# Two layer norms whose mean is taken off by matmuls with a centering matrix, in a four-block image kernel on one core

## Chip, cores and metric

The program runs on one core of one Trainium2 chip. It is one launch, and the metric is the device time in microseconds (us) of one execution. Engines: PE (TensorE, matmuls), DVE (VectorE), ACT (ScalarE), POOL (GpSimd), and SP, which here only issues DMAs. Each engine runs its own instructions in order and waits at semaphores for the others.

## What is computed

The input x has 8 images of 32 x 32 pixels and 64 channels (C). Four blocks follow, each added to x or taken from it after a group norm `_gn`. The third one matters here:

```python
def layer_norm(x, g, b, eps=1e-05):
    mu = jnp.mean(x, axis=-1, keepdims=True)
    var = jnp.var(x, axis=-1, keepdims=True)
    return (x - mu) / jnp.sqrt(var + eps) * g + b
...
x_norm = layer_norm(x_flat, ln_g, ln_b)          # over the 64 channels of a pixel
y = mamba_block(x_norm, in_proj_w, ..., out_proj_w)   # projections, selective scan, y @ out_proj_w.T
y = y + skip_scale * x_norm
y = layer_norm(y, ln_g, ln_b)
y = y @ proj_w.T + proj_b
...
x = x + _L0_conv_ref(_gn(x), ...)    # 5 steps of a diffusion with depthwise convolutions
x = x + _L1_conv_ref(_gn(x), ...)    # 3 x 3 convolution
x = x + _L2_conv_ref(_gn(x), ...)    # the block above
x = x + _L3_conv_ref(_gn(x))         # 2D DCT
```

So there are two layer norms over the channels: g = 0 ahead of the projections, and g = 1 behind the scan.

## The kernel before

Two images fill the 128 partitions (2 x 64 channels), a pair of images is a tile of 128 x 1024, and two pairs (k = 0 and 1) are worked on together as a half (h = 0 and 1). Data mostly lie with channels on partitions. Layer norms need sums over channels, so a tile is turned to pixels on partitions by eight 128 x 128 matmuls into PSUM; then each pixel's 64 channels lie in a row.

The order of every engine is written out by hand. In each half: the diffusion; a middle stage (convolution of k = 0 and 1 in four products each, `wino_product`; group norms; first layer norm; projections; causal convolution `causal`); then a loop over 64 scan steps s (`SCANS`), in which ACT makes exp(delta A) (`decay`), PE fills the scan's input in PSUM, DVE runs one scan of 128 x 1024 (L1775) and, in some steps, a product ahead of it (L1766), POOL multiplies by C (L389) and PE sums. Other work is hung into the steps by number. The second layer norm of k = 0 stands in steps 37 to 44; that of k = 1 is done in the next half's diffusion setup (half 0) or in a tail by halves of a tile (half 1).

One layer norm runs as follows, with the names of the code:

- PE brings the data to pixels. For g = 0 it is `n2_pixels`, eight transposes (L479 in the profile, through `transposes`) that signal `n2T`. For g = 1, `skip` and `out_proj` make the sum in PSUM and signal `mo`.
- DVE sums each pixel's channels (`center_sums`, L1519), the sum is divided by 64 (L1530 on DVE, or `small_mean` on ACT for g = 1), and DVE subtracts it in place in PSUM (L1532). This signals `xc`.
- ACT squares (`square`, signals `csq`), DVE sums the squares (`variance`, L1537) and signals, after a small step, `lvar`.
- POOL takes the power -1/2 (`layer_root`, L372; L463 in the tail) and signals `lrstd`; DVE multiplies (`normalize`, L1545).

Other lines named below: L1712 is `add_conv` (DVE, after the last two products of the convolution, L556 on PE); L1727 is the first instruction of `causal`, which waits for `x_in_proj` (L572 on PE); L581 is `z_in_proj`; L668 is `out_proj`; L502 is `depthwise`; L485 to L488 is `project`, here the last projection; L1783 is `add_block`, which adds that projection. L960 is the one helper through which all ACT operations go. L1956 to L1960 are the tail's mean and subtraction; L940 is the tail's last projection.

In the loop over the steps, ACT's list has `small_mean` at step 40 and `square` at step 41, DVE's has `center_sums` at 38, the subtraction at 39, `variance` at 41 and `normalize` at 43.

Of the kernel before, what the change touches and what calls it, by code (L numbers as in the profile page):

```python
# [6 lines left out]
ALU = mybir.AluOpType  # L7
# [8 lines left out]
P = 128  # L16
# [26 lines left out]
def fused_blocks(nc, x, vec, mats, conv_w, in_w, xbc_w, xdt_w, dtp_w, out_w, proj_w, out):  # L43
# [9 lines left out]
    with ctx:  # L53
# [27 lines left out]
        cpow = sb("cpow", 16)  # L81
        diag = sb("diag", 18 * P)
# [21 lines left out]
        for k in range(2):  # L104
# [117 lines left out]
        MIDDLE = ["add0", "add1", "sum0", "residual0", "sum1", "mean0", "residual1", "mean1"]  # L222
# [245 lines left out]
        def _(pe):  # L468
# [120 lines left out]
            def bc_proj(h, k):  # L589
                pe.wait_ge(S("par"), 1)  # L590
# [340 lines left out]
            pe.wait_ge(S("xc"), 4 * HALVES + 1)  # L931
# [26 lines left out]
        def _(act):  # L958
# [11 lines left out]
            act.wait_ge(S("par"), 7)  # L970
# [87 lines left out]
            def square(h, k, g):  # L1058
                act.wait_ge(S("xc"), 4 * h + 2 * g + k + 1)
# [110 lines left out]
            def small_mean(h, k):  # L1170
                m = D[k]["m"]
                act.wait_ge(S(f"lstep{k}"), 4 * h + 3)
                av(m[:, :], m[:, :], ACT.Identity, 1.0 / C).then_inc(S("lmean"), 1)

            def small_variance(h, k):
                v = D[k]["v"]
                act.wait_ge(S(f"lstep{k}"), 4 * h + 4)
# [55 lines left out]
            for h in range(HALVES):  # L1233
# [109 lines left out]
                for s in range(4, SCANS):  # L1343
# [60 lines left out]
            for n in range(2):  # L1404
                act.wait_ge(S("xc"), 4 * HALVES + n)
# [22 lines left out]
        def _(dve):  # L1428
# [9 lines left out]

            dve.wait_ge(S("vecs"), 16)
# [5 lines left out]
            ts(skipI[:, :], ident, vc("skip"), None, ALU.mult)  # L1445
# [18 lines left out]
            last.then_inc(S("par"), 1)  # L1464
            dve.wait_ge(S("bn_rstd"), 2)
            for n, (name, f) in enumerate([("g", DT), ("g1", DT), ("out", 1.0)]):
# [5 lines left out]
                dve.wait_ge(S("par"), 2 * n + 3)  # L1472
# [319 lines left out]
            for h in range(HALVES):  # L1792
# [16 lines left out]
                else:  # L1809
# [5 lines left out]
                    center(1, h - 1, 1)  # L1815
# [67 lines left out]
                center(0, h, 0)  # L1883
# [8 lines left out]
                center(1, h, 0)  # L1892
# [28 lines left out]
                for s in range(3, SCANS):  # L1921
# [8 lines left out]
                    if s == 38:  # L1930
# [134 lines left out]
```

## Time and profile before

| | us |
|---|---|
| median of 3 runs (lowest, highest) | 921.25 (920.52, 922.97) |
| the profiled execution, its own time | 922.08 |
| its span in the trace | 920.1 |
| setup until ACT's first large operation | 13.9 |
| middle stage and projections of half 0 | from 158 to 240 |
| scan of half 0, scan of half 1 | from 240 to 447, from 684 to 888 |
| tail after the last scan | from 888 to 920 |

The trace is of one execution. The span runs from its first to its last instruction; 1.98 us of its time lie around it. A timeline row gives start, duration, engine, line and operation; several like instructions in a row are merged and counted (x8), and what ended an idle time ahead stands in brackets. Neighbouring rows of DVE and ACT overlap by some 0.1 us.

### The profile page before, as it was taken

The numbers are of one execution on the slowest core, as the hardware profiler recorded it, in microseconds if no ns is written. First come the engines' busy times: TensorE is split into PE (matmuls) and PEld (weight loads), VectorE is DVE, ScalarE is ACT, GpSimd is POOL, SyncE is SP. The second block draws the span as 40 slices with busy tenths as digits, with TensorE's granted clock in tenths as the row PEclk, the third lists the DMA queues.
The fourth block names the chain that finished last, engine by engine and source line by source line (L and its number), as shares of the span: only waits on it lengthen the run. The fifth ranks groups of instructions, "written<-read, shape, count | busy, mean of one in ns | idle before, by whom it ended". The sixth has DMA issues, their size and how long they took to land. (4 is left out here: it accounts for less than half of the span.)

```text
span 920.1 us, 10656 instructions
## 1 busy us (share of the span) xinstructions
PE 751.1 (82%) x3890; PEld 505.2 (55%) x3890; DVE 820.1 (89%) x707; ACT 557.8 (61%) x961; POOL 523.1 (57%) x245
## 2 busy tenths in 40 slices
PE   3999999867777788688799899977778677868895
PEld 2344444434576678578655444434448567767873
DVE  6899887789999998999989978778999999899983
ACT  2774322237769898879477433223674978887922
POOL 3104998020489697778410199912047979777841
PEclk8899999899799999999899999989977999999998
DMA  3000000000635454345200200000033445535421
GB/s 112 1 0 0 0 0 0 1 0 3 183 124 183 150 182 173 137 165 191 58 0 1 69 1 0 0 0 1 0 103 128 167 163 183 189 132 184 173 80 24
DMA packets 33296, 75.03 MB, mean 82 GB/s; under 512 B 15708, under 2 KB 15844, under 8 KB 33248
## 3 DMA queue, kind: packets, MB, share of 16 engines
q1 hardware_dynamic: 31840, 73.09, 23.3%
q0 software_dynamic: 320, 1.05, 0.5%
q8 instruction: 29, 0.48, 0.2%
q10 hardware_dynamic: 1088, 0.26, 0.1%
q14 instruction: 19, 0.16, 0.1%
HBM read 70.71 MB, written 2.62 MB: 80 GB/s over the span
## 5 line engine op out<-in xcount | busy, mean ns | idle before, releaser
L389 POOL TENSOR_TENSOR arena<-arena 128x1024 f32<-128x1024 f32 x85 | 200.2, 2366 | 67.7 <-DVE arena L1775 63.3
L960 ACT ACTIVATE arena<-arena 128x128 f32<-128x128 f32 (+3 forms) x408 | 152.7, 448 | 93.1 <-DVE arena L1669 75.3
L1775 DVE TENSOR_TENSOR_SCAN arena<-arena,ps 128x1024 f32<-128x1024 f32 x86 | 194.7, 2277 | 9.1 <-ACT arena L960 6.8
L960 ACT ACTIVATE arena<-arena,Amat 128x1024 f32<-128x1024 f32 x128 | 143.3, 1141 | 8.4 <-DVE arena L1775 7.5
L646 PE MATMUL ps<-mat,arena 128*128 128x128 f32 x1016 | 137.2, 280 | 3.8 <-POOL arena L389 3.4
L605 PE MATMUL ps<-mat,arena 128*128 128x128 f32 x560 | 81.4, 293 | 64.5 <-DVE arena L1775 39.2
L960 ACT ACTIVATE arena<-ps 128x1024 f32<-128x1024 f32 (+2 forms) x65 | 56.0, 872 | 111.9 <-PE ps L479 46.7
L646 PEld LDWEIGHTS ps<-mat,arena 128*128 128x128 f32 x1016 | 119.1, 145 | 7.2 <-POOL arena L389 5.3
L389 POOL TENSOR_TENSOR arena<-HS,arena 128x1024 f32<-128x1024 f32 x42 | 99.8, 2377 | 28.2 <-DVE HS L1775 20.0
L605 PEld LDWEIGHTS ps<-mat,arena 128*128 128x128 f32 x560 | 65.8, 146 | 79.6 <-DVE arena L1775 49.1
L765 PE MATMUL ps<-arena,mat 128*128 128x512 f32 x240 | 106.3, 592 | 0.0
L1775 DVE TENSOR_TENSOR_SCAN HS<-arena,ps 128x1024 f32<-128x1024 f32 x42 | 95.6, 2277 | 2.4 <-ACT arena L960 1.7
L502 PE MATMUL ps<-arena,diag 128*128 128x512 f32 x180 | 83.4, 621 | 2.4 <-DVE ps L1580 2.4
L1766 DVE TENSOR_TENSOR ps<-arena,ps 128x1024 f32<-128x1024 f32 x70 | 84.7, 1210 | 0.0
L765 PEld LDWEIGHTS ps<-arena,mat 128*128 128x128 f32 x240 | 45.6, 190 | 57.4 <-issue 56.7
L502 PEld LDWEIGHTS ps<-arena,diag 128*128 128x128 f32 x180 | 35.3, 199 | 46.3 <-issue 42.8
L613 PE MATMUL ps<-mat,arena 128*128 128x128 f32 x304 | 40.2, 275 | 17.7 <-DVE arena L1775 13.4
L372 POOL TENSOR_TENSOR dr<-dv,cpow 128x16 f32<-128x16 f32 x7 | 20.9, 2988 | 56.8 <-DVE dv L1540 31.8
L960 ACT ACTIVATE ROWS<-arena 128x128 f32<-128x128 f32 x160 | 48.7, 390 | 0.0
L368 POOL TENSOR_TENSOR dgn<-dgn,cpow 128x1 f32<-128x1 f32 x12 | 7.4, 619 | 71.9 <-DVE dgn L1493 54.7
L437 POOL TENSOR_TENSOR arena<-arena 128x1024 f32<-128x1024 f32 x20 | 47.2, 2362 | 1.6
L378 POOL TENSOR_TENSOR arena<-arena 128x1024 f32<-128x1024 f32 x6 | 17.8, 2966 | 51.4 <-DVE arena L1742 51.4
(218 smaller groups left out, 1395.7 us busy)
## 6 DMA issues: line engine op xcount, KB each, us to landing
arena<-c_rows SPq DMA_DIRECT2D x128, 512.0 KB, 3.7
out<-arena SPq DMA_DIRECT2D x28, 64.0 KB, 2.2
xres<-x POOLq DMA_DIRECT2D x4, 256.0 KB, 5.3
xres<-x SPq DMA_DIRECT2D x4, 256.0 KB, 4.5
arena<-arena SPq DMA_DIRECT2D x4, 252.0 KB
convw<-conv_w SPq DMA_DIRECT2D x1, 576.0 KB
c_rows<-ROWS SPq DMA_DIRECT2D x4, 128.0 KB, 1.9
mat<-mats SPq DMA_DIRECT2D x1, 448.0 KB, 3.9
```

The source lines that it names most:

```text
L372: tt(t["r"][:, :], t["v"][:, :], cpow[:, :], ALU.pow).then_inc(S("lrstd"), 1)
L378: tt(du, du, two_images(j, "DL"), ALU.subtract).then_inc(S("spw"), 1)
L389: tt(HC[s % 2], HS[s % 3], CB[s % 4], ALU.mult).then_inc(S("hc"), 1)
L437: tt(a["G1"][:, :], a["R"], a["XY"], ALU.add).then_inc(S(f"a{k}_x"), 1)
L502: last = mm(half(conv_ps(h, k, w), n), blk(diag, 9 * (1 - w) + tap), frm(A[k]["fz"])[:, dy + HB * n:dy + HB * n + HB, dx:dx + W], start=Fa ...
L605: last = nc.tensor.transpose(blk(PS[s % 2], n), column.to_broadcast([P, P]), ident)
L613: last = nc.tensor.transpose(blk(PS[s % 2], n), tb_block(i, n), ident)
L646: last = mm(blk(PS[3], n), blk(HC[s % 2], n), ident, start=first and n % 4 == 0, stop=True, is_transpose=True, skip_group_check=True)
L765: last = mm(half(mix, n), mt(mname), half(a[src], n), start=False, stop=(name == "e"), skip_group_check=True)
L960: return nc.scalar.activation(out_, in_, func, bias=bias, scale=scale, accum_out=accum_out)
L1766: tt(PS[q][:, :], two_images(j, "DU"), PS[q][:, :], ALU.mult).then_inc(S("dbu"), 1)
L1775: nc.vector.tensor_tensor_scan(HS[s % 3], DA[s % 3], PS[q][:, :], 0.0, ALU.mult, ALU.add).then_inc(S("scan"), 1)
```

## The change

A matrix `centering`, for each image's 64 channels the identity less 1/64, is made once. Multiplying by it takes the mean over the channels off. It enters in three places.

- `n2_pixels` does eight plain matmuls with `centering` in place of eight transposes, so that PSUM holds centred values.
- `skipI` (the skip's diagonal) is made from `centering`, and the mean over the output channels is taken off `outw` in place. What `skip` and `out_proj` sum is then centred.
- `center_sums`, `center`, `small_mean` and the tail's loop over mean and subtraction go, with the tiles `m`. `square` waits for `n2T` or `mo` itself. In the scan it stands at step 39 (was 41), `variance` at 40 (was 41), `small_variance` at 42 (was 43). `normalize` and POOL's `layer_root` keep their places.

The core of the diff:

```diff
             def n2_pixels(h, k):
                 pe.wait_ge(S("n2"), 2 * h + k + 1)
-                transposes(D[k]["N2"], PS[2 * k]).then_inc(S("n2T"), 1)
+                for n in range(BLK):
+                    last = mm(blk(PS[2 * k], n), blk(D[k]["N2"], n), centering[:, :], start=True, stop=True, skip_group_check=True)
+                last.then_inc(S("n2T"), 1)
...
             spin(PS[0], 6)
-            pe.wait_ge(S("xc"), 4 * HALVES + 1)
+            pe.wait_ge(S("csq"), 4 * HALVES + 1)
...
             def square(h, k, g):
-                act.wait_ge(S("xc"), 4 * h + 2 * g + k + 1)
+                act.wait_ge(S(["n2T", "mo"][g]), 2 * h + k + 1)
...
                     first_tap(h, 1, 0)
-                    small_mean(h - 1, 1)
+                    square(h - 1, 1, 1)
                     frames(h, 1)
-                    square(h - 1, 1, 1)
...
-                    if s == 40:
-                        small_mean(h, 0)
-                    if s == 41:
+                    if s == 39:
                         square(h, 0, 1)
-                    if s == 43:
+                    if s == 42:
                         small_variance(h, 0)
...
+            dve.memset(centering[:, :], 0.0).then_inc(S("setup_step"), 1)
+            dve.wait_ge(S("setup_step"), 1)
+            chain[0] = 1
+            for b in range(2):
+                link(dve.memset(centering[C * b:C * b + C, C * b:C * b + C], -1.0 / C))
             dve.wait_ge(S("vecs"), 16)
...
-            ts(skipI[:, :], ident, vc("skip"), None, ALU.mult)
+            link(tt(centering[:, :], ident, centering[:, :], ALU.add))
+            ts(skipI[:, :], centering[:, :], vc("skip"), None, ALU.mult)
...
+            link(nc.vector.reduce_sum(par[:, 14:15], outw[:, :], axis=AX.X))
+            link(ts(par[:, 14:15], par[:, 14:15], 1.0 / C, None, ALU.mult))
+            ts(outw[:, :], outw[:, :], par[:, 14:15], None, ALU.subtract).then_inc(S("par"), 1)
...
-            def center(k, h, g, sums=True):
-                d, step, n0 = D[k], S(f"lstep{k}"), 4 * h + 2 * g
-                ps = PS[2] if g == 1 else PS[2 * k]
-                if sums:
-                    center_sums(k, h, g)
-                if g == 1:
-                    dve.wait_ge(S("lmean"), 2 * h + k + 1)
-                else:
-                    dve.wait_ge(step, n0 + 1)
-                    ts(d["m"][:, :], d["m"][:, :], 1.0 / C, None, ALU.mult).then_inc(S("mid_step"), 1)
-                    dve.wait_ge(S("mid_step"), middle(h, f"mean{k}"))
-                tt(v3(ps), v3(ps), d["m"][:, :].unsqueeze(2).to_broadcast([P, 16, C]), ALU.subtract).then_inc(S("xc"), 1)
...
                 wino_input(h, 1, 3)
                 wino_sums(h, 1)
-                center(0, h, 0)
                 add_residual(h, 1)
                 variance(0, h, 0)
...
-                center(1, h, 0)
                 causal(h, 0, 0, rest=False)
                 variance(1, h, 0)
...
-                    if s == 38:
-                        center_sums(0, h, 1)
-                    if s == 39:
-                        center(0, h, 1, sums=False)
-                    if s == 41:
+                    if s == 40:
                         variance(0, h, 1)
```

`link` runs an instruction and has DVE wait for its end. ACT's first wait is for `par` at 8 instead of 7, so it stands behind the new work on `outw`.

**DVE in the middle stage.** The instructions around the first layer norm of k = 0 in half 0 (arena1 is the convolution's data of k = 1, ps0 the pixels of k = 0, dm0 and dv0 its means and variances). Before:

```order
L1696 TENSOR_TENSOR arena1<-arena1,ps2 128x512
L1519 TENSOR_REDUCE dm0<-ps0 128x16
L1530 TENSOR_SCALAR dm0<-dm0 128x16
L1532 TENSOR_TENSOR ps0<-ps0,dm0 128x1024
L1703 TENSOR_TENSOR arena1<-arena1,xres1 128x512 x2
L1537 TENSOR_REDUCE dv0<-arena0 128x16
L1540 TENSOR_SCALAR dv0<-dv0 128x16
L1712 TENSOR_TENSOR arena1<-arena1,ps3 128x16x32 x2
```

Of the change:

```order
L1681 TENSOR_TENSOR arena1<-arena1,ps2 128x512
L1688 TENSOR_TENSOR arena1<-arena1,xres1 128x512 x2
L1522 TENSOR_REDUCE dv0<-arena0 128x16
L1525 TENSOR_SCALAR dv0<-dv0 128x16
L1697 TENSOR_TENSOR arena1<-arena1,ps3 128x16x32 x2
```

The sum, the division and the subtraction are gone. The addition of the residual now follows `wino_sums` directly, and the sum of squares comes next.

**DVE in the scan.** Steps 38 to 42 of half 0 (ps2 holds the second norm's sum for k = 0; L1775 is printed as another kind of instruction here than in the trace). Before:

```order
L1766 TENSOR_TENSOR ps0<-arena1,ps0 128x1024
L1775 SCALAR_TENSOR_TENSOR HS2<-arena1,ps0 128x1024
L1519 TENSOR_REDUCE dm0<-ps2 128x16
L1775 SCALAR_TENSOR_TENSOR arena0<-arena0,ps1 128x1024
L1532 TENSOR_TENSOR ps2<-ps2,dm0 128x1024
L1775 SCALAR_TENSOR_TENSOR arena0<-arena0,ps0 128x1024
L1766 TENSOR_TENSOR ps1<-arena1,ps1 128x1024
L1775 SCALAR_TENSOR_TENSOR HS2<-arena1,ps1 128x1024
L1537 TENSOR_REDUCE dv0<-arena0 128x16
L1775 SCALAR_TENSOR_TENSOR arena0<-arena0,ps0 128x1024
```

Of the change (L1760 is the scan, L1522 the sum of squares, L1751 the product ahead of a scan):

```order
L1751 TENSOR_TENSOR ps0<-arena1,ps0 128x1024
L1760 SCALAR_TENSOR_TENSOR HS2<-arena1,ps0 128x1024
L1760 SCALAR_TENSOR_TENSOR arena0<-arena0,ps1 128x1024
L1760 SCALAR_TENSOR_TENSOR arena0<-arena0,ps0 128x1024
L1522 TENSOR_REDUCE dv0<-arena0 128x16
L1751 TENSOR_TENSOR ps1<-arena1,ps1 128x1024
L1760 SCALAR_TENSOR_TENSOR HS2<-arena1,ps1 128x1024
L1760 SCALAR_TENSOR_TENSOR arena0<-arena0,ps0 128x1024
```

Between the scans of steps 38 and 40 nothing is left, and the sum of squares stands behind the scan of step 40 instead of that of step 41.

**ACT in the scan.** The same steps (rows with Amat are `decay`, rows of 128x128 the scaled inputs). Before:

```order
L960 ACTIVATE ROWS<-arena1,arena0 128x128 x8
L960 ACTIVATE arena0<-arena1,Amat 128x1024
L960 ACTIVATE dm0<-dm0 128x16
L960 ACTIVATE arena1<-arena1,Amat 128x1024
L960 ACTIVATE arena1<-arena1,arena0 128x128 x8
L960 ACTIVATE arena0<-ps2 128x1024
L960 ACTIVATE arena0<-arena1,Amat 128x1024
```

Of the change:

```order
L963 ACTIVATE ROWS<-arena1,arena0 128x128 x8
L963 ACTIVATE arena0<-ps2 128x1024
L963 ACTIVATE arena0<-arena1,Amat 128x1024
L963 ACTIVATE arena1<-arena1,Amat 128x1024
L963 ACTIVATE arena1<-arena1,arena0 128x128 x8
L963 ACTIVATE arena0<-arena1,Amat 128x1024
```

The square (arena0<-ps2) has moved ahead of the `decay` of step 40, behind which the scan of step 40 waits, and the small operation on dm0 is gone.

## Rows read from the trace of the kernel before

**Rows 1.** The page's busy times; share of the span; then two groups by line (columns as in the page).

```profile
PE 751.1 (82%) x3890; PEld 505.2 (55%) x3890; DVE 820.1 (89%) x707; ACT 557.8 (61%) x961; POOL 523.1 (57%) x245
...
L1519 DVE TENSOR_REDUCE dm<-ps 128x16 f32<-128x1024 f32 x7 | 8.6, 1225 | 10.6 <-PE ps L479 5.4 <-PE ps L668 5.2
...
L1532 DVE TENSOR_TENSOR ps<-ps,dm 128x1024 f32<-128x1024 f32 x7 | 8.6, 1225 | 0.7 <-ACT dm L960 0.6
```

**Rows 2.** Timeline of DVE and ACT, setup: start, us, engine, line, operation.

```profile
8.44 0.27 DVE L1445 TENSOR_SCALAR skipI<-mat,vecs 128x128 f32<-128x128 f32 x1
...
12.19 0.16 DVE L1469 TENSOR_TENSOR par<-vecs,par 128x1 f32<-128x1 f32 x1
...
13.92 1.94 ACT L960 ACTIVATE xres<-ps 128x1024 f32<-128x1024 f32 x2 [3.89 <-DVE par L1471]
```

**Rows 3.** Timeline of PE, middle of half 0.

```profile
183.12 5.32 PE L556 MATMUL ps<-arena,convw 128*128 128x512 f32 x12
...
195.46 1.09 PE L479 MATMUL ps<-mat,arena 128*128 128x128 f32 x8 [1.51 <-ACT arena L960]
...
196.55 1.98 PE L572 MATMUL ps<-arena,inw 128*128 128x512 f32 x4
...
198.37 1.95 PE L581 MATMUL ps<-inw,arena 128*128 128x128 f32 x16
```

**Rows 4.** Timeline of DVE, middle of half 0.

```profile
183.32 1.23 DVE L1519 TENSOR_REDUCE dm<-ps 128x16 f32<-128x1024 f32 x1 [0.26 <-PE ps L479]
...
187.14 1.21 DVE L1537 TENSOR_REDUCE dv<-arena 128x16 f32<-128x1024 f32 x1
...
188.47 1.28 DVE L1712 TENSOR_TENSOR arena<-arena,ps 128x512 f32<-128x512 f32 x2
...
196.59 1.22 DVE L1519 TENSOR_REDUCE dm<-ps 128x16 f32<-128x1024 f32 x1 [2.46 <-PE ps L479]
...
199.19 1.27 DVE L1727 TENSOR_SCALAR arena<-ps,vecs 128x1024 f32<-128x1024 f32 x1
```

**Rows 5.** Timeline of ACT, middle of half 0.

```profile
199.32 1.02 ACT L960 ACTIVATE arena<-ps 128x1024 f32<-128x1024 f32 x1 [2.82 <-DVE ps L1532]
```

**Rows 6.** Timelines of DVE, ACT, PE and POOL, scan steps 38 to 44 of half 1.

```profile
806.85 2.29 DVE L1775 TENSOR_TENSOR_SCAN HS<-arena,ps 128x1024 f32<-128x1024 f32 x1
...
810.14 1.23 DVE L1519 TENSOR_REDUCE dm<-ps 128x16 f32<-128x1024 f32 x1 [1.01 <-PE ps L668]
...
811.28 2.28 DVE L1775 TENSOR_TENSOR_SCAN arena<-arena,ps 128x1024 f32<-128x1024 f32 x1
...
828.09 2.28 DVE L1775 TENSOR_TENSOR_SCAN HS<-arena,ps 128x1024 f32<-128x1024 f32 x1
...
809.98 1.14 ACT L960 ACTIVATE arena<-arena,Amat 128x1024 f32<-128x1024 f32 x1
...
808.21 1.90 PE L668 MATMUL ps<-outw,arena 128*128 128x64 f32 x16
...
822.71 2.90 POOL L372 TENSOR_TENSOR dr<-dv,cpow 128x16 f32<-128x16 f32 x1
```

**Rows 7.** Timelines of PE and DVE, start of half 1, where the last norm of half 0 ends.

```profile
467.04 13.90 PE L502 MATMUL ps<-arena,diag 128*128 128x512 f32 x32
...
485.95 1.88 PE L488 MATMUL ps<-arena,projw 128*128 128x512 f32 x4
...
487.86 1.97 DVE L1783 SCALAR_TENSOR_TENSOR arena<-ps,vecs,arena 128x1024 f32<-128x1024 f32 x1 [0.66 <-PE ps L488]
```

**Rows 8.** Timelines at the end; the last row is a stretch, clock third from last.

```profile
892.65 0.69 DVE L1956 TENSOR_REDUCE dm<-ps 128x8 f32<-128x512 f32 x1 [1.94 <-PE ps L912]
...
896.67 3.24 POOL L463 TENSOR_TENSOR dr<-dv,cpow 128x8 f32<-128x8 f32 x2 [9.72 <-DVE dv L1966]
...
901.18 3.21 PE L940 MATMUL ps<-arena,projw 128*128 128x512 f32 x4
...
902.00:904.00 2.00, 2.00 (x3) 0.61 (x2) 1.09 (x1) 0.16 (x1) 0.00 (x0) 0.50 0.00 0
```

More of the change, by code:

```diff
@@ L81, in fused_blocks @@
         cpow = sb("cpow", 16)
+        centering = sb("centering", P)
         diag = sb("diag", 18 * P)
@@ L589, in bc_proj @@
             def bc_proj(h, k):
-                pe.wait_ge(S("par"), 1)
+                pe.wait_ge(S("par"), 2)
                 pe.wait_ge(S(f"xs{k}"), 2 * h + 2)
@@ L969, in _ @@
             av(Amat[:, :], vecs[:, V_ALOG:V_ALOG + D_STATE], ACT.Exp).then_inc(S("dtw"), 1)
-            act.wait_ge(S("par"), 7)
+            act.wait_ge(S("par"), 8)
             act.wait_ge(S("setup"), 3 + len(PE_TAPS) + 6)
@@ L1168, in keep_x @@
                 av(xres[k][:, :], ps[:, :], ACT.Identity).then_inc(S("a_x"), 1)
[L1170 to L1173, printed above, removed]
             def small_variance(h, k):
                 v = D[k]["v"]
-                act.wait_ge(S(f"lstep{k}"), 4 * h + 4)
+                act.wait_ge(S(f"lstep{k}"), 2 * h + 2)
                 av(v[:, :], v[:, :], ACT.Identity, 1.0 / C, par[:, 12:13]).then_inc(S("lvar"), 1)
@@ L1404, in _ @@
             for n in range(2):
-                act.wait_ge(S("xc"), 4 * HALVES + n)
+                act.wait_ge(S("mo"), 2 * HALVES + n)
                 av(half(F[1]["SQ"], n), half(PS[2], n), ACT.Square).then_inc(S("csq"), 1)
@@ L1513, in v3, with variance @@
                 return t[:, :].rearrange("p (g c) -> p g c", c=C)
-            def center_sums(k, h, g):
+            def variance(k, h, g):
                 d, step = D[k], S(f"lstep{k}")
-                ps = PS[2] if g == 1 else PS[2 * k]
-                dve.wait_ge(S(["n2T", "mo"][g]), 2 * h + k + 1)
-                nc.vector.reduce_sum(d["m"][:, :], v3(ps), axis=AX.X).then_inc(step, 1)
-            def center(k, h, g, sums=True):
-                d, step, n0 = D[k], S(f"lstep{k}"), 4 * h + 2 * g
-                ps = PS[2] if g == 1 else PS[2 * k]
-                if sums:
-                    center_sums(k, h, g)
-                if g == 1:
-                    dve.wait_ge(S("lmean"), 2 * h + k + 1)
-                else:
-                    dve.wait_ge(step, n0 + 1)
-                    ts(d["m"][:, :], d["m"][:, :], 1.0 / C, None, ALU.mult).then_inc(S("mid_step"), 1)
-                    dve.wait_ge(S("mid_step"), middle(h, f"mean{k}"))
-                tt(v3(ps), v3(ps), d["m"][:, :].unsqueeze(2).to_broadcast([P, 16, C]), ALU.subtract).then_inc(S("xc"), 1)
-            def variance(k, h, g):
-                d, step, n0 = D[k], S(f"lstep{k}"), 4 * h + 2 * g
                 dve.wait_ge(S("csq"), 4 * h + 2 * g + k + 1)
@@ L1538, in variance @@
                 if g == 0:
-                    dve.wait_ge(step, n0 + 2)
+                    dve.wait_ge(step, 2 * h + 1)
                     ts(d["v"][:, :], d["v"][:, :], 1.0 / C, LN_EPS, ALU.mult, ALU.add).then_inc(S("lvar"), 1)
@@ L1951, in _ @@
                 tt(sz, half(PS[3], n), sz, ALU.mult).then_inc(S("y_read"), 1)
-            for n in range(2):
-                m = groups(d["m"], n)
-                x = half(PS[2], n).rearrange("p (g c) -> p g c", c=C)
-                dve.wait_ge(S("mo"), 2 * HALVES + n)
-                nc.vector.reduce_sum(m, x, axis=AX.X).then_inc(S("lmean"), 1)
-                dve.wait_ge(S("lmean"), 2 * HALVES + 2 * n)
-                ts(m, m, 1.0 / C, None, ALU.mult).then_inc(S("lmean"), 1)
-                dve.wait_ge(S("lmean"), 2 * HALVES + 2 * n + 1)
-                tt(x, x, m.unsqueeze(2).to_broadcast([P, 8, C]), ALU.subtract).then_inc(S("xc"), 1)
             for n in range(2):
```

7 lines of the change are left out of this document (3 added, 4 removed).

## The prediction

> **What bounds the kernel now.** I read the page of the profile first: DVE is busy 89% of the span, PE 82%, ACT 61% [rows 1]. The eight removed pairs (seven whole ones by line, one by halves) are about 2.45 us of DVE each: 1.225 for the sum over channels and 1.225 for the subtraction, 17.2 us for the seven [rows 1]. That is the most a reader might hope for. The share of busy time doesn't tell what it is worth, so I then read the timelines of DVE at each place, with what ended its waits, and those of PE, ACT and POOL beside them. There are five places with different limits: setup, the middle stage (twice), the scan (twice), the start of half 1, and the tail.
>
> **Setup: +0.8 us.** DVE sets up constants without a gap until ACT starts at 13.92, after 3.89 us of waiting for DVE's last small instruction [rows 2]. New ahead of it, behind the arrival of the matrices: one 128x128 addition with a wait (the 128x128 multiplication takes 0.27, I take 0.3), and on outw a sum over 64, a division and a 64-wide subtraction (a 128x1 operation with its wait takes 0.16 and a little; I take 0.2, 0.2 and 0.1) [rows 2]. All lies on this path. The three memsets stand ahead of the wait for the first load, where DVE has nothing to do: 0. Bounds: 0.4 to 1.3.
>
> **Middle stage: +0.4 us in each half, though DVE loses 5 us of work there.** What the plain matmul costs on PE has a row: `z_in_proj`, also eight fp32 matmuls of 128x128 on 128x128, shows 16 records in 1.95 us; the eight transposes show 8 in 1.09 [rows 3]. So each turn takes 0.86 longer.
>
> First turn (k = 0). Now the turn ends, DVE sums at 183.32, and PE starts the last two products of the convolution at 183.12, which end at 183.12 + 5.32 = 188.44; the second `add_conv` needs that, and DVE begins the pair at 188.47 [rows 3, 4]. So PE is as late as DVE here. Removing some 2.6 us (1.23, a small step, 1.23) from DVE lets it run ahead to a wait, while PE's products end at 188.44 + 0.86 = 189.3. The second half of the pair, which begins 0.6 behind 188.47, i.e. at 189.07, then begins at about 189.35: +0.3.
>
> Second turn (k = 1). DVE waits 2.46 us for the turn, sums at 196.59, subtracts, and starts `causal` at 199.19 [rows 4]. `causal` needs `x_in_proj`, which is queued on PE right behind the turn and ends at 196.55 + 1.98 = 198.53 [rows 3]. So of the 2.6 us that the mean takes at most 0.66 was on the path. In the changed kernel the projection ends 0.86 later from the longer turn and 0.3 later from the first turn, less some 0.15 (it starts no earlier than its own input allows): about 199.55. `causal` starts 0.36 later than before; ACT's square (1.02 us, [rows 5]) comes earlier, but only `variance` behind `causal` wants it. From here DVE is without gaps through the four causal convolutions, so I carry +0.4 to the scan. Bounds from the same rows: -0.7 (all of the 0.66 comes off and PE is hidden) to +1.7 (both extra 0.86).
>
> The Trainium skill speaks against this edit. Its page Perfetto Trace Analysis (Optimizing Tensor Performance, Transposes) asks to use a transpose, not a standard matmul; TensorE: Matmul & The Clock Gate (Terms) gives the transpose mode as 4x faster for fp32. By that figure, an estimate from 4 x 1.09, a turn would take 4.4 us instead of 1.95, 2.4 more than I charge for each of four. The trace differs: 1.95 against 1.09 is a factor of 1.8 for this shape [rows 3].
>
> **Scan: -2.3 us in each half.** Before, the scan of step 38 ends at 806.85 + 2.29 = 809.14; DVE waits 1.01 for `mo` and sums at 810.14; step 39's scan starts at 811.28 [rows 6]. Step 39 needs nothing of that, its ACT and PE inputs are ready, so it moves to 809.05: 2.2 us. The subtraction behind it takes 1.1 more (1.225 less the overlap), [rows 1]. Together 3.3.
>
> What comes back: ACT finishes its scaled inputs at 809.98 and did `decay` 40 then, in 1.14 [rows 6]. Now the square stands ahead of it. It waits for `mo`, which ends at 808.21 + 1.90 = 810.11, takes 1.02 [rows 5] (0.9 until the next starts), so `decay` 40 ends at about 812.2. DVE is through with step 39 at 811.3 and stalls 0.95. Net 3.3 - 0.95 = 2.35. `normalize` at step 43 needs POOL's root, 2.90 us, at 822.71 before [rows 6]; it starts after the product of step 41, by my count at 821.5, and ends at 824.4, where DVE reaches `normalize` at 824.65: just in time. Behind it DVE remains the pace in my count (2.2 per scan, 1.1 to 1.2 per product or norm), so step 44 starts at 825.75 instead of 828.09 [rows 6] and the 2.3 stays. Both halves show the same pattern: -4.6. Bounds per half: 0 (another engine paces the scan) to -3.3 (no stall).
>
> **Start of half 1: 0.** DVE loses sum and subtraction of k = 1's second norm. But PE works through 16 convolution matmuls (32 records) from 467.04 for 13.90 us, to 480.9, before it can turn the normalised values, then through ten more and the last projection, which ends at 485.95 + 1.88 = 487.83; DVE waits for it with `add_block` at 487.86, already 0.66 us too early [rows 7]. DVE will be earlier by 1.3, and wait 1.3 longer. Bounds: 0 to -1.3.
>
> **Tail: -3.5 us.** Nothing else runs here, all is one path. Before, the first sum starts at 892.65 and POOL's root at 896.67, 4.02 later: sums, divisions, subtractions of both halves in turn, then the squares' sum [rows 8]. Changed: half a square (full one 1.02, [rows 5]; I take 0.6), half a sum 0.69 [rows 8], a small step, with hand-overs 1.6. That is -2.4. Further, the last projection takes 3.21 here, and the stretch from 902 shows a granted clock of 0.50, i.e. 1.2 instead of 2.4 GHz [rows 8], after PE had idled three times; the same four records at full clock take 1.88 [rows 7]. PE's spin matmuls will now join up with less idle time between, so I expect the clock to hold. The projection is needed half by half, so of the 1.33 I count 1.1. Bounds: -1.5 to -3.7.
>
> **Sum.** +0.8 + 0.8 - 4.6 + 0 - 3.5 = -6.5 on the profiled execution's own time of 922.08: 915.6. That execution lies 0.83 above the median of the runs, so the median comes to 914.8.
>
> **Rivals.**
> - A, the scan pays nothing: ACT or POOL paces it, and DVE's 2.3 us turn up as waits some steps later. For it: `normalize` follows the root by only 0.25 us in my count, and ACT's stall at step 40. Against it: ACT and POOL wait for DVE in most steps. Time: -6.5 + 4.6 = -1.9, i.e. 919.3. Chance 10%.
> - B, DVE's busy time counts in full, as on the busiest engine. Seven times 2.45 [rows 1], some 0.7 for four small steps and 3.1 in the tail (four of 0.69 and two small steps, [rows 8]) are 21; with +0.8 for setup the time is 901. The waits at 196.59 and 487.86 speak against it [rows 4, 7]. Chance 2%. The Trainium skill (Perfetto Trace Analysis, Identifying the Most-Contended Engine) has the engine with the highest occupancy optimised first; it adds that regimes differ, as they do here.
> - C, slower: PE's clock falls to 1.2 GHz in the middle stage, where PE is on the path. The last two products and the turn would take twice as long, 5.3 + 1.9 more per half, and the projections as much again: up to 13 more in each half. The tail shows that gaps do this [rows 8]. It decides from 9.3 us for both halves together (6.5 lost and 2.8 more). Against it: the change adds PE work there and no gap I can find, and the two products run at full clock (12 records in 5.32, [rows 3]). With only the convolution and turn affected: -6.5 + 14.4 = +7.9, about 929. Chance 4%.
> - D, a plain fp32 turn takes four times a transpose, 4 x 1.09 = 4.4 us instead of 1.95, and all of the 2.4 more comes on the path in each of the four turns: -6.5 + 9.6 = +3.1, i.e. 924.4. Chance 1%, since a row of the same shape stands against it [rows 3]. It is the factor of the page TensorE: Matmul & The Clock Gate of the Trainium skill.
>
> My forecast, with its own variants (clock in the tail falls anyway: 915.9; the start of half 1 gives 1.3: 913.5), has 83%. Its range is 912 to 918. A measurement here tells about 0.3%, 2.8 us, from no change. The range to hold 8 in 10, widened by half of rival A's loss: 911.5 to 919. Faster by over 0.3%: 0.85; within: 0.10; slower: 0.05.
>
> **What would show it.** DVE's first large instruction 0.8 later. In the middle, DVE waiting for PE with `add_conv` and 5 us ahead of `causal`, whose start is no earlier counted from the stage's begin. In the scan, no wait before step 39, about 0.95 for ACT before step 40, step 44 starting 2.3 earlier counted from step 38. At half 1's start a wait of about 2 us before `add_block`. In the tail, POOL's root 1.6 us behind `mo`, and L940's successor in 1.9 us. I would be wrong if the longer turn delays more than I see, or if a later wait in the scan takes the 2.3 back.

## The result and the profile after

The changed kernel takes 914.28 us (median of 7 runs, 912.94 to 917.23), against 920.52 (7 runs, 919.26 to 922.97) for the kernel before on the same chip. The ratio is 0.9937, 95% interval 0.9923 to 0.9951: 6.2 us less. The profiled execution took 914.04, its span is 912.1.

The page of the kernel after, its busy times:

```profile
PE 749.6 (82%) x3922; PEld 505.8 (55%) x3922; DVE 802.4 (88%) x690; ACT 557.9 (61%) x958; POOL 523.5 (57%) x245
```

Beside [rows 1], DVE has lost 17.7 us of work and the kernel 6.2. To see where they went I cut both executions at the same instructions of DVE and compare the stretches, from start to start. `wino_sums` is the last instruction of DVE ahead of the change in the middle stage; `gate` takes in the results of scan steps 0 to 15, 16 to 31 and 32 to 47, behind steps 17, 33 and 49.

| stretch, us | before | after | difference | predicted |
|---|---|---|---|---|
| start to ACT's first large operation | 13.92 | 14.80 | +0.88 | +0.8 |
| to `wino_sums` of half 0 (no code changed) | 168.47 | 166.05 | -2.42 | 0 |
| to the first `causal` | 16.80 | 17.16 | +0.36 | +0.4 |
| to the first `gate` | 103.54 | 104.58 | +1.04 | 0 |
| to the second `gate` | 49.20 | 49.19 | -0.01 | 0 |
| to the third `gate` | 51.69 | 49.41 | -2.28 | -2.3 |
| to `wino_sums` of half 1, with half 1's start | 219.49 | 219.67 | +0.18 | 0 |
| to the first `causal` | 16.80 | 17.16 | +0.36 | +0.4 |
| to the first `gate` | 103.01 | 102.66 | -0.35 | 0 |
| to the second `gate` | 49.14 | 49.15 | +0.01 | 0 |
| to the third `gate` | 51.69 | 49.40 | -2.29 | -2.3 |
| to the last scan | 41.90 | 41.95 | +0.05 | 0 |
| to the last copy | 28.77 | 25.29 | -3.48 | -3.5 |
| sum | 914.42 | 906.47 | -7.95 | -6.5 |

The six stretches for which the prediction has a term sum to -6.45; the medians differ by 6.24. The start of half 1, whose code changed too, lies in a stretch that shows +0.18. The rest of the profiles' difference stands in stretches whose work is the same, and there, as far as I followed it, it is PE's clock at the moment. Of the -2.42, 1.6 have come about by 50 us and the other 0.8 between 160 and 180. In the first of these places ACT waits for PE's depthwise products, which begin at 25.09 before and 25.97 after. Windows of before, then of after (busy time and records of PE stand first behind the length, the clock third from last):

```profile
26.00:29.00 3.00, 3.00 (x5) 1.35 (x4) 2.96 (x4) 2.97 (x4) 0.00 (x0) 0.50 0.00 0
29.00:32.00 3.00, 3.00 (x5) 1.05 (x5) 2.96 (x3) 2.94 (x7) 0.00 (x0) 0.64 0.00 0
32.00:35.00 3.00, 3.00 (x8) 1.32 (x7) 3.00 (x4) 1.02 (x1) 0.00 (x0) 1.00 0.00 0
```

```profile
26.00:29.00 3.00, 3.00 (x4) 1.41 (x5) 2.96 (x3) 2.97 (x5) 0.86 (x1) 1.00 0.00 0
29.00:32.00 3.00, 3.00 (x8) 1.32 (x7) 3.00 (x3) 2.97 (x4) 0.00 (x0) 1.00 0.00 0
```

A full stretch of 3 us holds 8 records of PE at full clock and 5 at half. The trace of after has no clock record before 28.8 us, so its 1.00 in the first window says nothing, and the 4 records there are those of half clock. What differs is when the full clock comes: 17.3 us behind ACT's first large operation before, by 14.0 after. Half of the difference is the 1.6. That a half clock was there isn't the price: g0_only (below) has it from 17.8 to 28.1 us, until 14.4 behind that operation, and is only 0.15 behind the changed kernel by 50 us.

**Setup.** DVE and ACT of the kernel after, timeline:

```profile
8.39 0.28 DVE L1445 TENSOR_TENSOR centering<-mat,centering 128x128 f32<-128x128 f32 x1
...
12.27 0.21 DVE L1466 TENSOR_REDUCE par<-outw 128x1 f32<-128x64 f32 x1
12.52 0.15 DVE L1467 TENSOR_SCALAR par<-par 128x1 f32<-128x1 f32 x1
12.71 0.26 DVE L1468 TENSOR_SCALAR outw<-outw,par 128x64 f32<-128x64 f32 x1
...
14.80 1.94 ACT L963 ACTIVATE xres<-ps 128x1024 f32<-128x1024 f32 x2 [5.01 <-DVE par L1475]
```

The new addition starts at 8.39, where `skipI` started at 8.44 before [rows 2]. From there to ACT it was 5.48 and is 6.41: +0.93.

**Middle stage.** PE and then DVE, half 0, of the kernel after:

```profile
180.66 2.05 PE L563 MATMUL ps<-centering,arena 128*128 128x128 f32 x16 [0.52 <-ACT arena L963]
182.55 5.32 PE L557 MATMUL ps<-arena,convw 128*128 128x512 f32 x12
...
194.21 2.05 PE L563 MATMUL ps<-centering,arena 128*128 128x128 f32 x16 [1.50 <-ACT arena L963]
196.09 1.88 PE L575 MATMUL ps<-arena,inw 128*128 128x512 f32 x4
```

```profile
183.81 1.22 DVE L1522 TENSOR_REDUCE dv<-arena 128x16 f32<-128x1024 f32 x1 [0.94 <-ACT arena L963]
...
187.90 0.69 DVE L1697 TENSOR_TENSOR arena<-arena,ps 128x512 f32<-128x512 f32 x1 [1.81 <-PE ps L557]
...
198.01 1.28 DVE L1712 TENSOR_SCALAR arena<-ps,vecs 128x1024 f32<-128x1024 f32 x1 [5.14 <-PE ps L575]
```

A turn takes 2.05 (16 records) where eight transposes took 1.09 [rows 3]. DVE's wait of 2.46 [rows 4] has become one of 5.14, and it waits 1.81 inside `add_conv` too. What was work of DVE is waiting for PE now.

**Scan.** DVE and ACT of the kernel after, half 1, steps 38 to 44 (L1760 is the scan):

```profile
804.62 2.29 DVE L1760 TENSOR_TENSOR_SCAN HS<-arena,ps 128x1024 f32<-128x1024 f32 x1
806.82 2.26 DVE L1760 TENSOR_TENSOR_SCAN arena<-arena,ps 128x1024 f32<-128x1024 f32 x1
810.06 2.29 DVE L1760 TENSOR_TENSOR_SCAN arena<-arena,ps 128x1024 f32<-128x1024 f32 x1 [0.98 <-issue]
...
822.45 1.20 DVE L1530 TENSOR_TENSOR arena<-ps,dr 128x1024 f32<-128x1024 f32 x1
823.57 2.28 DVE L1760 TENSOR_TENSOR_SCAN HS<-arena,ps 128x1024 f32<-128x1024 f32 x1
```

```profile
807.91 1.03 ACT L963 ACTIVATE arena<-ps 128x1024 f32<-128x1024 f32 x1
808.83 2.18 ACT L963 ACTIVATE arena<-arena,Amat 128x1024 f32<-128x1024 f32 x2
```

Step 39 follows step 38 without a wait. Before step 40 DVE stands 0.98. The profile puts that down to "issue"; the cause is in ACT's rows, where `decay` 40 is the first of the two at 808.83 and ends when DVE goes on, behind the square of 1.03. From step 38 to step 44 it was 21.24 [rows 6] and is 18.95: -2.29. `normalize` at 822.45 follows POOL's root by 0.24:

```profile
819.31 2.90 POOL L373 TENSOR_TENSOR dr<-dv,cpow 128x16 f32<-128x16 f32 x1
```

**Start of half 1.** DVE of the kernel after:

```profile
466.07 3.94 DVE L1565 SCALAR_TENSOR_TENSOR ps<-arena,vecs,ps 128x1024 f32<-128x1024 f32 x3 [4.85 <-ACT ps L963]
...
485.48 1.97 DVE L1768 SCALAR_TENSOR_TENSOR arena<-ps,vecs,arena 128x1024 f32<-128x1024 f32 x1 [1.64 <-PE ps L489]
```

The wait was 0.66 [rows 7]. Ahead of the sum DVE stood 3.18 for PE; now, without sum and subtraction, it stands 4.85 for ACT, so that of the 2.5 us removed 0.98 are left as longer waiting here, and nothing came of them: from the last `gate` of half 0 to this instruction it was 32.71 and is 32.74.

**Tail.** PE and POOL of the kernel after, and a window:

```profile
887.03 2.00 PE L915 MATMUL ps<-outw,arena 128*128 128x64 f32 x16
888.87 3.19 PE L517 MATMUL ps<-sel 96*128 96x512 bf16 x14
...
894.29 2.16 PE L943 MATMUL ps<-arena,projw 128*128 128x512 f32 x4
```

```profile
889.78 3.24 POOL L464 TENSOR_TENSOR dr<-dv,cpow 128x8 f32<-128x8 f32 x2 [7.31 <-DVE dv L1935]
```

```profile
894.00:896.00 2.00, 1.99 (x8) 0.78 (x6) 0.65 (x1) 0.78 (x1) 0.00 (x0) 1.00 0.00 0
```

POOL's root is 2.75 behind the start of `out_proj`, where it was 5.16: -2.41. From the root to the last copy it was 17.75 and is 16.69: -1.06, with the projection in 2.16 instead of 3.21 [rows 8].

### The profile page after: what moved, and what is told of

Read it like the earlier page. It is cut to its first block, busy times and chain, and to the rows that moved or that the text cites. A ratio compares the mean times of both kernels' runs of the same rounds, so it can differ in the third digit from the quotient of the medians.

```text
span 912.1 us, 10701 instructions
## 1 busy us (share of the span) xinstructions
PE 749.6 (82%) x3922; PEld 505.8 (55%) x3922; DVE 802.4 (88%) x690; ACT 557.9 (61%) x958; POOL 523.5 (57%) x245
## 4 chain that ended last, share of the span: by engine, by line
DVE 33%; PE 25%; ACT 18%; issue 15%; POOL 7%; DMA 1%; SPq 1%; POOLq 0%; DVEq 0%; ACTq 0%
ACT arena L963 15%; PE ps L768 6%; DVE ps L1751 5%; DVE arena L1760 5%; PE ps L557 4%; PE ps L503 4%; DVE HS L1760 3%; DVE arena L1715 3%; POOL arena L435 2%; POOL arena L436 2%; PE ps L762 2%; ACT ROWS L963 2%; POOL arena L438 1%; PE ps L649 1%; PE ps L671 1%
## 5 line engine op out<-in xcount | busy, mean ns | idle before, releaser
L1760 DVE TENSOR_TENSOR_SCAN arena<-arena,ps 128x1024 f32<-128x1024 f32 x86 | 194.7, 2277 | 9.8 <-ACT arena L963 5.6
L649 PEld LDWEIGHTS ps<-mat,arena 128*128 128x128 f32 x1016 | 117.3, 144 | 9.8 <-POOL arena L390 7.9
L608 PEld LDWEIGHTS ps<-mat,arena 128*128 128x128 f32 x560 | 65.0, 145 | 80.2 <-DVE arena L1760 45.9
L1760 DVE TENSOR_TENSOR_SCAN HS<-arena,ps 128x1024 f32<-128x1024 f32 x42 | 95.7, 2277 | 2.5 <-ACT arena L963 1.7
L1751 DVE TENSOR_TENSOR ps<-arena,ps 128x1024 f32<-128x1024 f32 x70 | 84.8, 1211 | 0.0
L379 POOL TENSOR_TENSOR arena<-arena 128x1024 f32<-128x1024 f32 x6 | 17.8, 2962 | 53.5 <-DVE arena L1727 53.5
```

The costliest lines, as they stand in the source:

```text
L608: last = nc.tensor.transpose(blk(PS[s % 2], n), column.to_broadcast([P, P]), ident)
L649: last = mm(blk(PS[3], n), blk(HC[s % 2], n), ident, start=first and n % 4 == 0, stop=True, is_transpose=True, skip_group_check=True)
L1751: tt(PS[q][:, :], two_images(j, "DU"), PS[q][:, :], ALU.mult).then_inc(S("dbu"), 1)
L1760: nc.vector.tensor_tensor_scan(HS[s % 3], DA[s % 3], PS[q][:, :], 0.0, ALU.mult, ALU.add).then_inc(S("scan"), 1)
```

## The experiments

Each ratio is to the kernel before on the same chip. Executions of one kernel lie up to 5 us apart and the intervals are about 3 us wide. Differences to the changed kernel are between medians of different rounds, in part of different chips (the kernel before had 920.13 to 920.52 there), so those under some 2 us aren't clear of noise. Small steps are read from the stretches of the table above, each in one profiled execution.

After the result one reading stood against mine. There are four `causal` per half: two of k = 0, then two of k = 1. From the first of k = 0 to the first of k = 1 the time had grown from 12.88 to 13.89 in both halves; below this is "`causal` to `causal`". PE's rows there and the window of the kernel after:

```profile
205.64 1.37 PE L480 MATMUL ps<-mat,arena 128*128 128x128 f32 x8 [2.72 <-DVE arena L1530]
206.80 3.34 PE L489 MATMUL ps<-arena,dtw 128*128 128x512 f32 x4
```

```profile
206.00:208.00 2.00, 2.00 (x9) 1.48 (x8) 1.96 (x2) 0.95 (x1) 0.00 (x0) 0.58 0.00 0
```

The clock falls there to 0.58, behind a wait of 2.72, and the same four records that take 1.88 at full clock [rows 7] take 3.34. **Theory 1** (my prediction's): the change costs 0.36 per half in the middle, pays 2.3 per half in the scan and 3.5 in the tail, and the rest is where the clock happens to be. **Theory 2**: the change itself makes the clock fall in the middle, and costs some 1 us more per half.

**g1_only: the middle stage as before, only the second norm centred by weights**

```diff
-for n in range(BLK):
-    last = mm(blk(PS[2 * k], n), blk(D[k]["N2"], n), centering[:, :], ...)
+transposes(D[k]["N2"], PS[2 * k]).then_inc(S("n2T"), 1)
...
+center(0, h)   # sum, division and subtraction, as before
 add_residual(h, 1)
...
+center(1, h)
 causal(h, 0, 0, rest=False)
```

> Only the second layer norm is centred by TensorE; the first has its transposes, sums and subtractions back. Theory 1 (the ledger of the prediction): the first norm's part costs 0.36 us per half directly, so this kernel is 0.7 faster than the changed one, about 913.5. Theory 2 (the clock): in the changed kernel's trace PE's clock falls behind a gap of 2.72 us ahead of the turn to channels and costs 1.0 more per half; then this one is 2.7 faster, about 911.6, and the clock stays at 1.00 there as in the trace of before. Rival (the subtraction's busy time counts): slower than the changed one by up to 10, 924. In the trace, from DVE's last wino_sums to its first causal instruction: 16.8 us (17.2 in the changed kernel).

Measured: 914.14, ratio 0.9926 (0.9911 to 0.9941). `wino_sums` to `causal` is 16.82 in both halves, as before the change, and `causal` to `causal` 12.88. But from the fourth `causal` to the first `gate` it is 84.68 in half 0, where it was 83.14 before: the time that is not lost at one place is lost at the next. 0.14 under the changed kernel is nearer theory 1 (0.7 expected) than theory 2 (2.7).

**g0_only: the kernel before with only the first norm centred by the turn**

```diff
-transposes(D[k]["N2"], PS[2 * k]).then_inc(S("n2T"), 1)
+for n in range(BLK):
+    last = mm(blk(PS[2 * k], n), blk(D[k]["N2"], n), centering[:, :], ...)
...
-center(0, h, 0)
-center(1, h, 0)
```

> The counterpart: only the first layer norm is centred by TensorE, the second is as before. Theory 1: setup +0.3, middle +0.36 per half: 921.5 against 920.5 of before. Theory 2 (clock falls as well): +3.0, 923.5. Rival (removed DVE time counts): 10 us faster than before, 911. In the trace the same 17.2 us from wino_sums to the first causal instruction, and a granted clock near 0.5 for some 3 us behind the turn of k = 1 to channels if theory 2 holds.

Measured: 922.95, ratio 1.0030 (1.0018 to 1.0043), slower than before. The stretches are 17.16 in the middle, twice, 51.70 in the scan, and 28.86 in the tail, as each theory has them. So this half of the change only costs. But the 2.5 us (1.7 to 4.0 by the interval) are more than the 1.0 of theory 1 (0.36 twice and the addition in setup), which lies outside; theory 2's 3.0 lies inside. The 12 runs scatter from 921.3 to 925.7, and I have no row for the rest: in the profiled execution `causal` to `causal` is 13.89 twice, but from the first `causal` to the first `gate` the two halves together take 0.66 more than before, not 2.

**spin_middle: ten bf16 matmuls on PE in the wait of 2.72, their result unused**

```diff
 x_in_proj(h, 0, 1)
+spin(PS[3], 10)
 xn_channels(h, 1)
```

> The changed kernel with ten more spin matmuls (results unused) on PE in the gap of 2.72 us between the projections of k = 0 and the turn of k = 1 to channels. If the clock falls because of that gap, it holds now and DVE's causal convolution of k = 1 doesn't wait 0.9 for PE: 2.0 faster than the changed kernel, 912.3. If the fall at that place was a matter of one execution: no difference, 914.3. If PE is in the way of its own turn: slower by up to 1.

Measured: 914.84, ratio 0.9939 (0.9925 to 0.9953). PE of this kernel at the same place:

```profile
203.04 2.32 PE L517 MATMUL ps<-sel 96*128 96x512 bf16 x10
205.92 1.09 PE L480 MATMUL ps<-mat,arena 128*128 128x128 f32 x8 [0.56 <-DVE arena L1531]
206.85 1.88 PE L489 MATMUL ps<-arena,dtw 128*128 128x512 f32 x4
```

The clock holds, the four records take 1.88 and `causal` to `causal` 12.87 and 12.89. The time is no better: from the fourth `causal` to the first `gate` it is now 84.47 and 82.48, where the changed kernel has 83.15 and 81.23. The clock falls later instead. A window of this kernel, then of the changed one:

```profile
224.00:228.00 4.00, 4.00 (x6) 1.06 (x5) 3.93 (x5) 2.59 (x3) 0.27 (x1) 0.57 0.00 0
```

```profile
224.00:228.00 4.00, 3.62 (x8) 1.01 (x8) 3.93 (x5) 3.56 (x4) 0.00 (x0) 1.00 0.00 0
```

So theory 2's loss is there as a row, and where it is prevented another takes its place.

**square_late: the square one step later on ACT, behind the `decay` of step 40**

```diff
-if s == 39:
+if s == 40:
     square(h, 0, 1)
```

> The changed kernel with ACT's square of the second norm at step 40 instead of 39, so that decay 40 doesn't stand behind it. If the stall of 0.98 ahead of step 40's scan comes from ACT's order, it goes, nothing takes its place (variance wants the square only behind step 40's scan), and each half gains 0.95: 1.9 faster than the changed kernel, about 912.4. If the stall has another source (the wait is put down to issue in the trace), it stays: 914.3. From the scan of step 38 to that of step 44: 18.0 us instead of 18.95 on the one theory, 18.95 on the other.

Measured: 912.76 (912.47 to 913.36), ratio 0.9916 (0.9901 to 0.9931), 1.5 under the changed kernel by medians, 2.2 by the two stretches below. ACT and DVE of this kernel, the same steps of half 1:

```profile
807.59 1.14 ACT L963 ACTIVATE arena<-arena,Amat 128x1024 f32<-128x1024 f32 x1
808.63 1.00 ACT L963 ACTIVATE arena<-ps 128x1024 f32<-128x1024 f32 x1
```

```profile
806.66 4.44 DVE L1760 TENSOR_TENSOR_SCAN arena<-arena,ps 128x1024 f32<-128x1024 f32 x2
```

Steps 39 and 40 are one group without a wait, and second to third `gate` takes 48.32 in both halves, 1.09 less than 49.41. So the wait that the profile called "issue" was made by ACT's order.

**scan_back: the mean's sum and subtraction put back into the scan for k = 0**

The values are centred already, so this takes off a mean that is near zero; it is only the work and the order of before.

```diff
-if s == 40:
+if s == 38:
+    center_sums(h)
+if s == 39:
+    center(h)
+if s == 41:
     variance(0, h, 1)
```

> The changed kernel with the scan's sum, small operation and subtraction back at steps 38 to 40, square and variance at step 41, in both halves (again on values that are centred already). Theory: each half's stretch between the gates of steps 33 and 49 goes from 49.4 back to 51.7, total 4.6 more, 918.9. Rival (the gain came from elsewhere, for one the order of ACT's square): less than 2 more.

Measured: 918.64, ratio 0.9982 (0.9969 to 0.9994), 4.4 over the changed kernel. Second to third `gate` is 51.70 and 51.69, within 0.01 of before; all other stretches that the change touched stay as changed. DVE waits for `mo` again, 1.00 where it was 1.01 [rows 6]:

```profile
810.00 1.23 DVE L1531 TENSOR_REDUCE dm<-ps 128x16 f32<-128x1024 f32 x1 [1.00 <-PE ps L671]
```

**half1_back: the same for k = 1, at half 1's start**

```diff
+center(h - 1)   # sum over channels and subtraction, on centred values
...
-square(h - 1, 1, 1)
+small_mean(h - 1, 1)
 frames(h, 1)
+square(h - 1, 1, 1)
```

> The changed kernel with DVE's sum and subtraction of k = 1's second norm, ACT's small operation and the old order on ACT put back at the start of half 1 alone (the values are centred already, so this only costs time). Theory: PE paces this stretch, the 2.5 us of DVE are hidden, the stretch from the gate to the addition of the last projection stays 32.7 us and its wait shrinks from 1.64 to 0.66: 914.3. Rival: they count, 1.3 to 2.5 slower.

Measured: 914.31, ratio 0.9947 (0.9928 to 0.9965), the time of the changed kernel. DVE waits 0.66 before `add_block`, as before [rows 7], PE is the one that is late, and from the `gate` to `add_block` it takes 32.19, no longer than 32.74:

```profile
484.89 1.96 DVE L1784 SCALAR_TENSOR_TENSOR arena<-ps,vecs,arena 128x1024 f32<-128x1024 f32 x1 [0.66 <-PE ps L489]
```

**setup_late: DVE's new setup work behind the first group norms**

```diff
-link(tt(centering[:, :], ident, centering[:, :], ALU.add))
-...
+# the same five instructions, behind group_norms(A, 0, 0)
-act.wait_ge(S("par"), 8)
+act.wait_ge(S("par"), 7)
```

> The changed kernel with DVE's new setup work (the addition of the identity, skipI, and the three operations on outw) moved from ahead of ACT's start to behind the first group norms, where DVE next waits 1.00 us for ACT's first tap; PE waits once, long after, for it. If the setup's cost was 0.8 on the path, ACT's first large operation starts 0.8 earlier, and the work fits into that wait: 0.8 faster than the changed kernel in that stretch (total 913.5, which the scatter of the runs hardly tells). If setup is paced by the arriving weights, nothing moves.

Measured: 912.93 (912.79 to 913.21), ratio 0.9924 (0.9906 to 0.9943), 1.35 under the changed kernel. ACT of this kernel:

```profile
13.23 2.12 ACT L965 ACTIVATE xres<-ps 128x1024 f32<-128x1024 f32 x2 [3.30 <-DVE par L1472]
```

The matrices from HBM arrived 0.51 earlier here (DVE's first instruction on them starts at 4.65, in the changed kernel's profile at 5.16). Counted from there ACT starts after 8.58 instead of 9.64: 1.06 of setup came back, some 0.2 of it for `skipI`, which moved with the rest (8.70 to 8.90 in the changed kernel).

**before_spin: the kernel before, its three groups of 6, 4 and 4 filler matmuls in the tail made one of 23**

```diff
-spin(PS[0], 6)
-pe.wait_ge(S("xc"), 4 * HALVES + 1)
-spin(PS[0], 4)
-pe.wait_ge(S("lvar"), 4 * HALVES + 1)
-spin(PS[0], 4)
+spin(PS[0], 23)
```

> The kernel before, whose 14 spin matmuls in the tail (6, 4 and 4 with waits between) are replaced by 23 without waits, some 5.6 us in one piece, up to the turn of the normalised values. Theory: this alone keeps PE's clock up, the last projection takes 1.9 to 2.2 instead of 3.2, and the tail from the last scan to the last copy goes from 28.8 to 27.7: 1.1 faster than before, 919.4. Rival (the clock falls for another reason, or its fall hid under DVE): no change.

Measured: 919.81, ratio 0.9998 (0.9986 to 1.0009). PE of this kernel in the tail, and a window on its projection:

```profile
891.85 5.13 PE L516 MATMUL ps<-sel 96*128 96x512 bf16 x23
897.61 0.66 PE L906 MATMUL ps<-mat,arena 128*128 128x128 f32 x4 [0.63 <-DVE arena L1966]
899.21 0.66 PE L906 MATMUL ps<-mat,arena 128*128 128x128 f32 x4 [0.95 <-DVE arena L1966]
899.71 2.16 PE L936 MATMUL ps<-arena,projw 128*128 128x512 f32 x4
```

```profile
901.00:903.00 2.00, 0.86 (x2) 0.04 (x1) 1.96 (x2) 0.00 (x0) 0.00 (x0) 1.00 0.00 0
```

In the trace the clock's share is isolated: the tail falls from 28.77 to 27.73, 1.04 against my term of 1.1. In the medians it can't be told from nothing: the interval holds both 0 and 1.04. This kernel, without any part of the change, also shows 13.89 from `causal` to `causal` in half 1, behind a wait of 2.04. So the row on which theory 2 rests doesn't need the change, though it is more frequent with it (see the table further down).

**no_tail_spin: the changed kernel without filler matmuls in the tail**

```diff
-spin(PS[0], 6)
-...
-spin(PS[0], 4)
```

> The changed kernel without the tail's 14 spin matmuls and the two waits between them. If they are what keeps the clock up, it is at 1.2 GHz for the last projection: that takes 3.2 us or more instead of 2.16 and the tail 26.4 to 27 instead of 25.3; 915.5. If the shorter tail does it without them: no change.

Measured: 918.15, ratio 0.9973 (0.9961 to 0.9984); nine of ten runs lie between 917.3 and 918.6, one at 913.85. PE in the tail, and a window:

```profile
893.30 0.88 PE L909 MATMUL ps<-mat,arena 128*128 128x128 f32 x4 [3.16 <-DVE arena L1934]
894.90 1.12 PE L909 MATMUL ps<-mat,arena 128*128 128x128 f32 x4 [0.72 <-DVE arena L1934]
895.81 3.62 PE L938 MATMUL ps<-arena,projw 128*128 128x512 f32 x4
```

```profile
896.00:899.00 3.00, 3.00 (x5) 0.78 (x3) 1.09 (x1) 0.78 (x1) 0.00 (x0) 0.50 0.00 0
```

POOL's root stands 2.74 behind the start of `out_proj` (890.88 after 888.14), as in the changed kernel, but the tail takes 28.31 instead of 25.29: 3.02 for a clock at half from the turns of the normalised values on (0.88 and 1.12 instead of 0.66 twice). I had expected 1.2 in all; what stands behind the projection is slow as well. So without the fillers, which are older than the change, the changed tail would lose 3.0 us by the trace, 3.9 by the medians.

**plain_turn: the kernel before with its turn as a plain matmul by the identity, nothing removed**

```diff
-transposes(D[k]["N2"], PS[2 * k]).then_inc(S("n2T"), 1)
+for n in range(BLK):
+    last = mm(blk(PS[2 * k], n), blk(D[k]["N2"], n), ident, ...)
+last.then_inc(S("n2T"), 1)
```

> The kernel before with its eight transposes of the first norm's turn replaced by eight plain matmuls by the identity, nothing else. It measures the turn's price alone. Theory: 16 records in 1.95 to 2.05 us instead of 8 in 1.09, all of the 0.86 to 0.95 on the path for both turns since DVE's sum waits for them: from wino_sums to the first causal instruction 18.5 us instead of 16.8, 3.4 more in all, 923.7. Rival (a plain fp32 turn takes four times a transpose, 4.4 us): 23.4 us in that stretch, 13 more in all, 933.

Measured: 925.53, ratio 1.0061 (1.0044 to 1.0078). PE of this kernel, half 0, then half 1:

```profile
195.76 2.05 PE L562 MATMUL ps<-mat,arena 128*128 128x128 f32 x16 [1.50 <-ACT arena L962]
...
636.88 3.78 PE L562 MATMUL ps<-mat,arena 128*128 128x128 f32 x16 [0.89 <-ACT arena L962]
```

At full clock a turn takes 2.05, and `wino_sums` to `causal` 18.72, 1.92 more than 16.80: both turns' 0.96 lie on the path when DVE's work isn't removed. In half 1 the clock had fallen ahead of the turn and the same stretch took 20.46. The two sum to 5.6, near the 5.4 measured. So in the middle stage the removed 5 us of DVE pay 1.56 (18.72 to 17.16), and the turn that removes them costs 1.92. Rival D's factor of four is not there: 2.05 against 1.09 is 1.9, in the kernel of before and in that of after. The Trainium skill (TensorE: Matmul & The Clock Gate, Terms) gives four for fp32; the measurement decides, and it is less than half of that for this shape. Its advice against turning with a standard matmul (Perfetto Trace Analysis, Optimizing Tensor Performance, Transposes) the trace does support here, with 925.53 against 920.13.

**combined: g1_only with square_late and setup_late**

> What the experiments point to: only the second norm centred by TensorE (the first norm as before), ACT's square at step 40, setup's new work behind the first group norms. From the stretches measured: setup 0.9, middle 2 x 0.36, scan 2 x 1.09 less than the changed kernel, together 3.8: 910.5. If the parts hide each other or the clock falls more often, 912 to 913.

Measured: 911.42 (910.69 to 911.71), ratio 0.9908 (0.9891 to 0.9924), 8.7 under the kernel before and 2.9 under the changed one. Each stretch is as in its own experiment: 16.82 and 16.81 in the middle, 48.32 twice in the scan, 25.30 in the tail. The medians of the parts give 0.14 + 1.52 + 1.35 = 3.0, close to the 2.9. I had expected 910.5; what is missing is nearly what g1_only's median lacked too, 0.7 expected and 0.14 seen.

## Why the prediction held, step by step

- **Setup, predicted +0.8**: +0.93 by rows. From start to start the addition takes 0.31 (0.3 predicted), and sum, division and subtraction 0.61 (12.27 to 12.88), for which I took 0.5.
- **Middle stage, +0.4 per half**: +0.36 in every kernel with the centering turn and without it 0 (g1_only, combined). The steps held: DVE waits 1.81 inside `add_conv` and 5.14 ahead of `causal`, and the turn is 0.96 longer where I took 0.86.
- **Scan, -2.3 per half**: -2.28 and -2.29; the stall before step 40 0.98 for 0.95 predicted; `normalize` 0.24 behind the root for 0.25. scan_back undoes it and square_late takes the stall away. Rival A falls with them.
- **Start of half 1, 0**: half1_back costs nothing. DVE came earlier by 0.98, not 1.3.
- **Tail, -3.5**: -3.48, of it -2.41 path (predicted -2.4) and -1.06 clock (predicted -1.1). I had POOL's root 1.6 behind `mo`: ACT's square starts on the first half's `mo` at 888.17 and the root at 889.78, 1.6 later. before_spin and no_tail_spin show the clock's part; the path's part has no experiment of its own, only the rows and the tails of g0_only (28.86) and g1_only (25.30).
- **Rival B** (busy time counts in full, 901) falls: 17.7 us less of DVE's busy time gave 6.2.
- **Rival C** (clock falls in the middle): the convolution's products (5.32) and turns (2.05) ran at full clock. A clock fall was there 10 us later, and of 1 us. The stretch from the first `causal` to the first `gate` of half 0 lies between 103.55 and 105.53, mean 104.5, in the seven kernels with the centering turn and no fillers there, and between 103.53 and 105.08, mean 104.2, in the other six; in half 1 the means are 102.7 and 102.7. What moves is the place of the fall, as the table below has it: the change lengthens PE's wait from 2.0 to 2.7 us and brings the fall forward. A cost of that isn't seen in these traces; g0_only's median speaks for one.
- **The sum** was -6.5; the changed stretches sum to -6.45, the medians differ by 6.24. The time, 914.8 against 914.28, hangs on the kernel before as well: the forecast took it from three runs with a median of 921.25, and seven have 920.52, from which the sum gives 914.0. It put the clock in unchanged code at nothing, and in the medians it was about that; this was assumed and not derived. The profiled executions differ by 8.0, of which 1.5 lie in stretches for which the sum has no term.

Where PE's clock fell to half between the first `causal` and the first `gate`, counted from the first `causal`, in halves of the profiled executions, one per kernel:

| place of the fall | centering turn, no fillers there (7 kernels, 14 halves) | transposes (4 kernels, 8 halves) | first `causal` to first `gate`, half 0, us |
|---|---|---|---|
| some 8 us behind, as PE's wait ends | 11 | 1 | 104.6, once 105.5 |
| some 26 us behind | 1 | 4 | 104.9 to 105.1 |
| neither | 2 | 3 | 103.5 to 103.6 |

spin_middle has it at 26 us in both halves; plain_turn, whose PE waits 0.64 and 1.52 us there, fits neither column.

Open: at which gaps the clock falls in a given execution; whether its earlier fall in the middle costs anything in the medians; and 1.4 of g0_only's 2.5.

## What to carry to other kernels

Removed work pays what its engine is late at that place, and DVE's 2.45 per norm paid 2.3, about 0.8 and nothing at three places of one kernel: read the wait that ends last at each. Price the instruction that takes over on the engine behind it, with its queue; the turn's 1.92 on PE ate more than the 1.56 that DVE gave. On an engine that runs in order, put the removed chain's next instruction behind the one that the pace-maker waits for (the square behind `decay`, 1.09 per half for one moved line).

## What the runs showed of the hardware

- A plain fp32 matmul of 128x128 shows as two records, a transpose as one: eight take 2.05 and 1.09 (plain_turn and the kernel before, full clock).
- A wait of 2.0 to 2.7 us on PE in mid-kernel was followed by a fall of the granted clock in some executions and not in others with the same code there. Ten fillers that cut it to 0.56 kept the clock at that place; it fell to 0.57 some 18 us later instead, and the time stayed the same.
- In the tail, where nothing else covers it, the clock counts: 3.02 in the tail without fillers. Nine runs of that kernel took about 918 and one 913.85; what made the one isn't shown (its mean granted clock, 0.957, is like the others').
